# One index table, an unchecked first index, a wait before the second-layer weight requests, and nine warm-up products

## The chip, the cores and the metric

The kernel runs on one core of one Trainium2 chip. The metric is the device time in microseconds of one execution, the median of several. TensorE (PE) does the matrix products; VectorE (DVE), ScalarE (ACT) and GpSimd (POOL) prepare operands and empty the result banks; SyncE (SP) and ScalarE issue the DMA requests, and the profile lists what their queues do as SPq and ACTq.

## The reference

For each of the two samples b, x is 1024 tokens by 256 features. Each sample picks one of 64 weight matrices for layer 0, and one of 3 expert MLPs for layer 1; two further MLPs are shared.

```python
x = x + (einsum('bsd,bdh->bsh', x, W[cat_ids]) + b[cat_ids][:, None, :])
s0, s1 = relu(x @ swi[0]) @ swo[0], relu(x @ swi[1]) @ swo[1]
eo = relu(x @ wi[type_label]) @ wo[type_label]          # type_label: one of 3 per sample
gate_in = concatenate([eo[:, 0], s0[:, 0], s1[:, 0]], axis=-1)
w = softmax(relu(gate_in @ g1) @ g2, axis=-1)[:, :, None, None]
x = x + eo * w[:, 0] + s0 * w[:, 1] + s1 * w[:, 2]
```

## The kernel before

Everything lies feature-major: 128 partitions hold features, 512 tokens are one tile's columns, and a sample has two tiles (t) of two feature halves (d). A product in f32 accuracy is made of three products of rounded operands: high by high, high by low and low by high. So each operand is first rounded (`x_hi`, `w_hi`, `m_hi`, `h_hi`, mostly by ACT), and the remainder is then taken (`x_lo`, `w_lo`, `m_lo`, `h_lo`, by DVE or POOL). Nothing is scheduled by a compiler: each engine's instructions stand in a written order, and semaphores hold the engines together.

**TensorE's order.** `WARMUP` = 10 products of `ones` into the bank `left` (L912), which nobody reads; `layer0_first` (sample 0, tile 0: 12 products of 512 columns), `layer0(0, 1)` (12 more, both on L739); `direct_first` (the first group of the MLP's hidden units, L782); `direct(1, i)` (the second group, L730, i = 0 to 3 into left, chain, corner, right); `layer0(1, 0)` and `layer0(1, 1)`; eight `output(0, u)`; and then the long loop over groups 2 to 23. `direct(1, i)` waits for `h_lo` number i of group 0, for they share a bank. `output(0, 4)` starts a bank that `make_x1(1, 1, 0)` on DVE must have emptied (L508).

**SP's order.** It loads the first index (`value_load`, L237, a read of a table in device memory), issues two requests for layer 0's weights `w_raw` and one for the bias (`load_layer0(0)`); loads the first expert index (L246); requests the weights of group 0 (`wo`) and group 1 (`wi`, `wo`), 256 KB each (L194, L201); requests sample 1's four halves of x, 256 KB each (L188, `load_x(sp, 1, t, d)`); and then does `load_layer0(1)`. From group 2 on it waits for a staging buffer to come free.

**ACT's order.** It requests x's first half (0, 0, 0), loads the expert index for itself (L410), and requests (0, 0, 1); once the first half has landed, it requests x's second tile, (0, 1, 0) and (0, 1, 1); it rounds `w_hi`, requests group 0's `wi` (L194), and goes on rounding. In the stretch that the prediction speaks of, its order is `hidden_hi(0, 0)`, `x_hi_of(1, 0, 0)`, `hidden_hi(0, 1)`, `x_hi_of(1, 0, 1)`, `hidden_hi(0, 2)`, `split_first_hi(0, True)`, `hidden_hi(0, 3)`, `w_hi_of(1, d)`. `x_hi_of` waits until that half of x has landed.

**DVE's order.** After `hidden_lo(0, i)` come `w_lo_of(1, d)`, `x_lo_of(1, 1, d)`, `make_x1(1, 0, 0)`, `hidden_lo(1, 0)`, `make_x1(1, 0, 1)`, `hidden_lo(1, 1 to 3)`, `make_x1(1, 1, 0)`, `make_x1(1, 1, 1)`.

Of the kernel before, what the change touches and what calls it, by code (L numbers as in the profile page):

```python
# [14 lines left out]
DC = 2  # L15
SHARED = 2
GROUPS = 4
DIRECT = 2
WARMUP = 10
SLOTS = 3  # L20

SQ = 32
# [21 lines left out]
NTH = [1, 3, 2, 4]  # L44

def build(nc, x_t, cat_w, cat_b, mlp_w, mlp_ids, cat_ids, g1, g2, out_t):
    B, _, _, S = x_t.shape
    D = DC * P
    HALVES = S // TOK  # L50
    CATS = cat_w.shape[0]
    BANKS = mlp_w.shape[0]
    EXPERTS = BANKS - SHARED
    assert B == 2 and HALVES == 2

    with ExitStack() as ctx:
# [6 lines left out]
        def sem(name):  # L63
            return ctx.enter_context(nc.semaphore(name))
# [57 lines left out]
        x_loaded = [[[sem(f"x_loaded{b}{t}{d}") for d in range(DC)] for t in range(HALVES)] for b in range(B)]  # L122
# [49 lines left out]
        def x1_part(b, t, d):  # L172
            return x1[:, b, t, d, :]
# [13 lines left out]
        def load_x(eng, b, t, d):  # L187
            eng.dma_start(x1_part(b, t, d), x_t[b][:, d, t * TOK:(t + 1) * TOK]).then_inc(x_loaded[b][t][d], 16)  # L188
# [7 lines left out]
        def load_group(eng, bank, j):  # L196
            if j < DIRECT:

                if j:
                    load_wi(eng, bank, j)  # L200
                eng.dma_start(staged[:, j % 2, WO:A11], group_weights(bank, j, slice(WO, A11))).then_inc(wo_loaded[j], 16)  # L201
            else:
                eng.dma_start(staged[:, j % 2, 0:RAW_S], group_weights(bank, j, slice(0, RAW_S))).then_inc(staged_loaded[j % 2], 16)
# [10 lines left out]
        def second_part(j):  # L214
            return DIRECT + j + 1 if j < DIRECT else 2 * j + 2
# [18 lines left out]
        @block.sync  # L234
        def _(sp):
            def load_layer0(b):
                cat = sp.value_load(cat_ids[0:1, b:b + 1], min_val=0, max_val=CATS - 1)  # L237
                for d in range(DC):
                    sp.dma_start(w_raw[:, b, d * D:(d + 1) * D], cat_w[bass.ds(cat, 1), :, d].rearrange("a p n -> p (a n)")  # L239
                                 ).then_inc(w_loaded[b][d], 16)  # L240
                sp.dma_start(bias[:, b, :], cat_b[bass.ds(cat, 1)].rearrange("a p d -> p (a d)")).then_inc(bias_loaded[b], 16)

            load_layer0(0)
            for q, (kind, _) in enumerate(PASSES):
                if kind == 0:
                    mlp = sp.value_load(mlp_ids[0:1, q:q + 1], min_val=0, max_val=EXPERTS - 1)  # L246
                    bank = bass.ds(mlp, 1)
                else:
                    bank = slice(EXPERTS + kind - 1, EXPERTS + kind)
                for j in range(q * GROUPS, (q + 1) * GROUPS):  # L250
                    if j >= 2:

                        sp.wait_ge(m_split, second_part(j - 2))
                    load_group(sp, bank, j)
                    if j == 1:
                        for t in range(HALVES):
                            for d in range(DC):
                                load_x(sp, 1, t, d)
                        load_layer0(1)
                if q == 0:  # L260

                    sp.wait_ge(layer0_done, B * HALVES * DC)
                    sp.dma_start(g1_sb[:], g1).then_inc(g_loaded, 16)
                    for d in range(DC):
                        sp.dma_start(g2_sb[:, d, :, :], g2[:, d, :].rearrange("(a c) k -> c a k", c=SQ)).then_inc(g_loaded, 16)

            for b in range(B):
                sp.wait_ge(added[b][0], 3)
                sp.dma_start(out_t[b, :, :, 0:TOK], x1[:, b, 0, :, :]).then_inc(out_written, 16)
            for n, (b, t) in enumerate(PAIRS[PASSES[-1][1]]):  # L270
                for d in range(DC):
                    sp.wait_ge(last_added, n * DC + d + 2)
                    columns = slice(0, TOK // 2 if n * DC + d == 2 * DC - 1 else TOK)
                    sp.dma_start(out_t[b, :, d, t * TOK:(t + 1) * TOK][:, columns], x1_part(b, t, d)[:, columns]
                                 ).then_inc(out_written, 16)
            sp.wait_ge(out_written, 16 * (B + 2 * DC + 1))
# [70 lines left out]
        def _(act):  # L347
# [59 lines left out]

            act.wait_ge(ones_ready, 1)
            nc.scalar.activation(table[:], ones[:, 0:1], ACT.Relu)
            mlp = act.value_load(mlp_ids[0:1, 0:1], min_val=0, max_val=EXPERTS - 1)  # L410

            load_x(act, 0, 0, 1)
            act.wait_ge(x_loaded[0][0][0], 16)
# [35 lines left out]
            for j in range(DIRECT, N):  # L449
# [21 lines left out]
                q = j // GROUPS - 1  # L471
# [24 lines left out]
            b, t = PAIRS[PASSES[-1][1]][1]  # L496
# [229 lines left out]
        def _(pe):  # L726
# [183 lines left out]
            pe.wait_ge(ones_ready, 1)  # L910
            for _ in range(WARMUP):
                nc.tensor.matmul(left[:, 0:P], ones[:], ones[:], start=True, stop=True)  # L912
# [72 lines left out]
```

## Time and profile before

| | before |
|---|---|
| device time, median of 3 runs | 268.43 us (268.33 to 268.64) |
| the profiled execution, its own time | 268.28 us |
| its span, first to last instruction | 266.4 us |
| TensorE busy | 262.2 us, 98% of the span |
| weight loads (PEld), DVE, ACT, POOL busy | 217.4, 162.7, 150.0, 162.1 us |
| share of TensorE in the chain that ended last | 97% |
| granted TensorE clock, mean | 1.000 |

The profiled execution's time is 1.9 us more than its span. A row of the timeline is: start, duration, engine, line, operation, what is written from what, shapes, and in brackets the idle time of the engine before it with what ended that. Instructions of an engine overlap a little in these rows, because each is shown from its start to the end of its last write.

### The profile page before, as it was taken

To read this page: it belongs to the slowest core of one execution; us is meant where nothing else is said; L and a number is where in the kernel's file an instruction comes from. 1 tells how busy PE (TensorE), PEld (TensorE's weight loads), DVE (VectorE), ACT (ScalarE), POOL (GpSimd) and SP (SyncE) were. 2 spreads that over 40 slices of the span, in tenths; PEclk is the share of its full clock that TensorE was granted. 3 is DMA by queue.
4 is the path that set the end of the run, shared out by engine and by line. 5 is a ranking of instruction groups with operands and counts; after the bars stand their busy time and mean duration, and the time that the engine had idled before them with its cause. 6 is when DMAs were issued, how large, how long until landed. Compare 5 with 4: busy or idle time off the path is not lost.

```text
span 266.4 us, 3466 instructions
## 1 busy us (share of the span) xinstructions
PE 262.2 (98%) x1160; PEld 217.4 (82%) x1160; DVE 162.7 (61%) x246; ACT 150.0 (56%) x266; POOL 162.1 (61%) x171
## 2 busy tenths in 40 slices
PE   8999999999999999999999999999999999999995
PEld 7788888888888888888888888888888888888884
DVE  3879968635645435644445565345477577985664
ACT  2696357866666555565655744646645755645320
POOL 0379999999958949838944725725626528535000
PEclk9999999999999999999999999999999999999999
DMA  5844322112012112202022112012022022000404
GB/s 154 235 162 160 119 79 80 28 55 80 16 65 79 38 41 79 79 5 79 0 81 79 20 58 81 9 73 79 2 79 79 0 79 80 1 0 0 157 4 158
DMA packets 7473, 18.31 MB, mean 69 GB/s; under 512 B 1312, under 2 KB 2080, under 8 KB 7456
## 3 DMA queue, kind: packets, MB, share of 16 engines
q1 hardware_dynamic: 6592, 16.65, 18.7%
q10 hardware_dynamic: 864, 1.44, 1.7%
q8 instruction: 9, 0.15, 0.2%
q14 instruction: 8, 0.07, 0.1%
HBM read 16.00 MB, written 2.10 MB: 68 GB/s over the span
## 4 chain that ended last, share of the span: by engine, by line
PE 97%; DMA 1%; SPq 1%; issue 0%; DVE 0%; ACT 0%; DVEq 0%
PE acc L730 49%; PE chain L730 23%; PE right L730 12%; PE left L730 6%; PE acc L739 4%; DMA w_raw<-cat_w 1%; SPq L237 1%; PE left L782 1%; PE corner L730 1%; PE right L782 1%; PE corner L782 1%; PE chain L782 1%; DVE x L721 0%; ACT w_hi L373 0%; SPq L239 0%
## 5 line engine op out<-in xcount | busy, mean ns | idle before, releaser
L281 POOL TENSOR_TENSOR m_lo<-staged,m_hi 128x512 fp32r<-128x512 f32 (+2 forms) x49 | 82.9, 1702 | 76.3 <-ACT m_hi L361 62.8
L730 PE MATMUL acc<-h_hi,m_hi 128*128 128x512 f32 x190 | 73.9, 389 | 0.0
L730 PE MATMUL acc<-h_hi,m_lo 128*128 128x512 f32 x190 | 73.9, 389 | 0.0
L730 PE MATMUL acc<-h_lo,m_hi 128*128 128x512 f32 x190 | 73.9, 389 | 0.0
L385 ACT COPY kept<-chain 128x512 f32<-128x512 f32 x66 | 38.9, 589 | 52.8 <-PE chain L730 52.7
L730 PEld LDWEIGHTS acc<-h_lo,m_hi 128*128 128x128 f32 x190 | 35.7, 188 | 7.5
L730 PEld LDWEIGHTS acc<-h_hi,m_lo 128*128 128x128 f32 x190 | 35.7, 188 | 7.4
L730 PEld LDWEIGHTS acc<-h_hi,m_hi 128*128 128x128 f32 x190 | 35.7, 188 | 7.3
L517 DVE SCALAR_TENSOR_TENSOR h_lo<-left,h_hi 128x512 fp32r<-128x512 f32 x24 | 16.6, 690 | 28.4 <-ACT h_hi L397 28.4
L281 POOL TENSOR_TENSOR staged<-staged 128x128 f32<-128x128 f32 x66 | 30.9, 482 | 1.7
L522 DVE TENSOR_TENSOR left<-left,kept 128x512 f32<-128x512 f32 x22 | 15.3, 694 | 23.7 <-PE left L730 23.7
L517 DVE SCALAR_TENSOR_TENSOR h_lo<-corner,h_hi 128x512 fp32r<-128x512 f32 x24 | 16.6, 691 | 16.3 <-ACT h_hi L397 16.3
L522 DVE TENSOR_TENSOR corner<-right,kept 128x512 f32<-128x512 f32 x22 | 15.4, 699 | 17.9 <-ACT kept L385 17.9
L730 PE MATMUL chain<-t_hi,m_lo 128*128 128x512 f32 x66 | 25.7, 389 | 0.0
L730 PE MATMUL chain<-t_hi,m_hi 128*128 128x512 f32 x66 | 25.7, 389 | 0.0
L730 PE MATMUL chain<-t_lo,m_hi 128*128 128x512 f32 x66 | 25.7, 389 | 0.0
L397 ACT ACTIVATE h_hi<-right 128x512 fp32r<-128x512 f32 x24 | 14.4, 600 | 19.2 <-DVE right L522 18.8
L397 ACT ACTIVATE h_hi<-corner 128x512 fp32r<-128x512 f32 x24 | 14.4, 600 | 18.5 <-DVE corner L522 18.5
L361 ACT CAST m_hi<-staged 128x896 fp32r<-128x896 f32 x22 | 20.8, 944 | 0.0
L517 DVE SCALAR_TENSOR_TENSOR h_lo<-right,h_hi 128x512 fp32r<-128x512 f32 x24 | 16.6, 691 | 3.5 <-ACT h_hi L397 0.8
L281 POOL TENSOR_TENSOR t_lo<-t_raw,t_hi 128x512 fp32r<-128x512 f32 x12 | 15.3, 1298 | 2.5 <-ACT t_hi L404 2.5
L517 DVE SCALAR_TENSOR_TENSOR h_lo<-chain,h_hi 128x512 fp32r<-128x512 f32 x24 | 16.3, 680 | 0.4 <-ACT h_hi L397 0.4
(149 smaller groups left out, 439.0 us busy)
## 6 DMA issues: line engine op xcount, KB each, us to landing
staged<-mlp_w SPq DMA_DIRECT2D x22, 512.0 KB, 3.3
x<-x_t ACTq DMA_DIRECT2D x4, 256.0 KB, 3.4
x<-x_t SPq DMA_DIRECT2D x4, 256.0 KB, 6.9
out_t<-x SPq DMA_DIRECT2D x2, 512.0 KB, 4.4
staged<-mlp_w SPq DMA_DIRECT2D x3, 256.0 KB, 3.6
g_sb<-g SPq DMA_DIRECT2D x1, 768.0 KB, 3.8
out_t<-x SPq DMA_DIRECT2D x3, 256.0 KB, 2.3
w_raw<-cat_w SPq DMA_DIRECT2D x4, 128.0 KB, 2.9
```

Of the source, the lines that this page charges most:

```text
L237: cat = sp.value_load(cat_ids[0:1, b:b + 1], min_val=0, max_val=CATS - 1)
L281: return nc.gpsimd.tensor_tensor(out, a, b, ALU.subtract)
L361: nc.scalar.copy(m_hi[:, j % SLOTS, 0:PLAIN], staged[:, j % 2, 0:PLAIN]).then_inc(m_hi_ready, 1)
L385: nc.scalar.copy(kept[:, n, :], chain[:]).then_inc(kept_ready, 1)
L397: nc.scalar.activation(h_hi[:, j % 2, i, :], hidden[i][:], ACT.Relu).then_inc(h_hi_ready, 1)
L517: nc.vector.scalar_tensor_tensor(out=h_lo[:, j % 2, i, :], in0=hidden[i][:], scalar=0.0, in1=h_hi[:, j % 2, i, :].bitcast(F32), op0=ALU.ma ...
L522: nc.vector.tensor_tensor(out[:], product[:], kept[:, n, :], ALU.add).then_inc(hidden_ready, 1)
L730: last = nc.tensor.matmul(out[:, columns], half[:, slot, at:at + P], moving[:, columns], start=(start and n == 0), stop=(stop and n == 2), ...
L739: return nc.tensor.matmul(acc[t][d][:], w[:, b, at:at + P], x_part(x, b, t, i), start=start, stop=stop)
L782: return nc.tensor.matmul(hidden[i][:], w[:, 0, at:at + P], moving, start=start, stop=stop, skip_group_check=True)
```

## The change

One table `ids` holds the two layer-0 indices and then the two expert indices, in place of `cat_ids` and `mlp_ids`, and the expert indices are now read at a nonzero offset. The layer-0 index is loaded without bounds. SP waits for the second half of x's second tile before its first request for group 0's weights, and with it before all its further requests. There are 9 warm-up products in place of 10.

```diff
-WARMUP = 10
+WARMUP = 9
...
             def load_layer0(b):
-                cat = sp.value_load(cat_ids[0:1, b:b + 1], min_val=0, max_val=CATS - 1)
+                cat = sp.value_load(ids[0:1, b:b + 1])
...
                 if kind == 0:
-                    mlp = sp.value_load(mlp_ids[0:1, q:q + 1], min_val=0, max_val=EXPERTS - 1)
+                    mlp = sp.value_load(ids[0:1, B + q:B + q + 1], min_val=0, max_val=EXPERTS - 1)
...
                 for j in range(q * GROUPS, (q + 1) * GROUPS):
+                    if j == 0:
+
+                        sp.wait_ge(x_loaded[0][1][DC - 1], 16)
                     if j >= 2:
...
-            mlp = act.value_load(mlp_ids[0:1, 0:1], min_val=0, max_val=EXPERTS - 1)
+            mlp = act.value_load(ids[0:1, B:B + 1], min_val=0, max_val=EXPERTS - 1)
...
-        "mlp_ids": np.asarray(itok_B_0_2)[None],
-        "cat_ids": np.asarray(itok_B_0_63)[None],
+
+        "ids": np.concatenate([np.asarray(itok_B_0_63), np.asarray(itok_B_0_2)])[None],
```

## Rows read from the trace of the kernel before

**Rows 1.** The page: the span in 40 slices, TensorE and its clock.

```profile
PE   8999999999999999999999999999999999999995
PEclk9999999999999999999999999999999999999999
```

**Rows 2.** The chain of work that ended last, by time: start, length, what.

```profile
2.49 0.05 SPq L239
...
2.65 2.57 DMA w_raw<-cat_w
...
5.25 0.41 ACT w_hi L373
...
5.79 5.88 PE acc L739 x24
```

**Rows 3.** Line L237 from 0 to 3 us: duration ns least/median/most, start.

```profile
L237 SPq TENSOR_LOAD <-cat_ids_ptr x1: 859/859/859, 0.7 to 0.7; - x1
L237 SPq TENSOR_LOAD <-cat_ids x1: 524/524/524, 1.6 to 1.6; - x1
L237 SPq FUSED_REGOPS  x1: 181/181/181, 2.2 to 2.2; - x1
L237 SPq SEQ_ASSERT  x1: 28/28/28, 2.4 to 2.4; - x1
```

**Rows 4.** Line L246, the expert index on SP, whole span.

```profile
L246 SPq TENSOR_LOAD <-mlp_ids_ptr x2: 1448/1690/1933, 4.2 to 29.4; - x2
L246 SPq ALU_OP  x1: 41/41/41, 31.3 to 31.3; - x1
```

**Rows 5.** The timeline, 6.7 to 9 us, layer 0's operands and SP's requests.

```profile
6.73 0.69 DVE L504 TENSOR_TENSOR x_lo<-x,x_hi 128x512 fp32r<-128x512 f32 x1
7.38 0.34 SPq L201 DMA_DIRECT2D staged<-mlp_w  x1
7.74 0.62 PE L739 MATMUL acc<-x_lo,w_hi 128*128 128x512 f32 x2
8.28 0.62 ACT L369 CAST x_hi<-x 128x512 fp32r<-128x512 f32 x1 [0.28 <-DMA x<-x_t]
```

**Rows 6.** Line L912, the warm-up, whole span.

```profile
L912 PE MATMUL left<-ones x20: 341/421/579, 1.1 to 5.3; 128*128 128x128 f32 x20
```

**Rows 7.** Line L201 at 8.4 us, group 1's `wo`: its request and landing.

```profile
L201 SPq DMA_DIRECT2D staged<-mlp_w x1: 332/332/332, 8.4 to 8.4; - x1
...
DMA to landing us min/median/max: 4.0/4.0/4.0
```

**Rows 8.** Line L188 at 8.8 us, sample 1's first half of x, likewise.

```profile
L188 SPq DMA_DIRECT2D x<-x_t x1: 432/432/432, 8.8 to 8.8; - x1
...
DMA to landing us min/median/max: 6.7/6.7/6.7
```

**Rows 9.** Windows of 1 us: PE, PEld, DVE, ACT, POOL, clock, DMA share, GB/s.

```profile
12.00:13.00 1.00, 1.00 (x6) 0.84 (x5) 1.00 (x2) 0.39 (x1) 0.52 (x1) 1.00 0.73 123
```

**Rows 10.** The timeline, 14.4 to 18.3 us: the way from x to `direct(1, 1)`.

```profile
14.40 0.62 ACT L354 CAST m_hi<-staged 128x512 fp32r<-128x512 f32 x1
14.92 0.59 ACT L397 ACTIVATE h_hi<-left 128x512 fp32r<-128x512 f32 x1
15.49 0.62 ACT L369 CAST x_hi<-x 128x512 fp32r<-128x512 f32 x1
16.02 0.59 ACT L397 ACTIVATE h_hi<-chain 128x512 fp32r<-128x512 f32 x1
16.64 0.69 DVE L517 SCALAR_TENSOR_TENSOR h_lo<-chain,h_hi 128x512 fp32r<-128x512 f32 x1 [0.41 <-ACT h_hi L397]
18.11 0.19 PEld L730 LDWEIGHTS chain<-part_hi,m_hi 128*128 128x128 f32 x1
```

**Rows 11.** The timeline, 28.9 to 30.4 us: the way to `output(0, 4)`.

```profile
28.91 0.74 DVE L508 SCALAR_TENSOR_TENSOR x<-acc,bias,x 128x512 f32<-128x512 f32 x1
30.34 0.19 PEld L730 LDWEIGHTS acc<-h_hi,m_hi 128*128 128x128 f32 x1
```

More of the change, by code:

```diff
@@ L44, with build @@
 NTH = [1, 3, 2, 4]
-def build(nc, x_t, cat_w, cat_b, mlp_w, mlp_ids, cat_ids, g1, g2, out_t):
+def build(nc, x_t, cat_w, cat_b, mlp_w, ids, g1, g2, out_t):
     B, _, _, S = x_t.shape
@@ L50, in build @@
     HALVES = S // TOK
-    CATS = cat_w.shape[0]
     BANKS = mlp_w.shape[0]
```

## The prediction

> **What bounds the kernel now.** I read the page first: TensorE is at nine tenths or more in every slice between the first and the last, and its clock column is full throughout [rows 1]. So no other engine bounds it; time can be won or lost only where TensorE starts, where it pauses, and at the end. The chain of waits says the same with times: it is SP's work and a transfer of `w_raw` up to 5.22 us, a cast on ACT from 5.25 to 5.66, and from 5.79 TensorE to the end [rows 2]. The change touches the way to 5.79 and the order of the transfers behind it. A 128x512 product follows the last after 0.227 us (the row at 7.74 has two that end 0.62 later, 0.39 being one's own length [rows 5]). The 24 products of layer 0's first sample take 5.88 us [rows 2] where 24 x 0.227 = 5.45, so some 0.4 us of pauses lie in that stretch. After that I find none: whatever comes late by less than its slack costs nothing, whatever comes later shifts the whole rest.
>
> **The first index without its assertion.** SP reads a pointer (0.859 us), reads the index (0.524), then runs a FUSED_REGOPS of 0.181 and a SEQ_ASSERT of 0.028 [rows 3]; its address arithmetic starts at 2.49 and the request goes out at 2.65 [rows 2]. The read ends at about 0.73 + 0.86 + 0.03 + 0.52 = 2.14. Without the last two, the arithmetic can start at 2.18, which saves 0.31. The lower bound is 0.07 (SEQ_ASSERT and its gap alone, if the FUSED_REGOPS were needed); I take 0.31, since the address arithmetic has an instruction of its own at 2.49. `w_raw` would then land at 4.91, `w_hi` be done at 5.35, and the first product start at 5.48, 0.31 earlier.
>
> **One table.** Line L246 reads its pointer twice, once per load, from the same table [rows 4], so a load never reuses a pointer that the queue has read; one table saves no read. What it adds is an offset: the expert load at offset 0 has no ALU_OP, the one at offset 1 has one of 41 ns [rows 4], about 0.08 us with its gaps. Both expert loads at 4.2 us and on ACT now get one. On SP it is hidden behind the new wait. On ACT it stands ahead of the request of x's half (0, 0, 1), which then lands 0.08 later, or 0.2 to 0.3 later if layer 0's second `w_raw` request, now sent first, takes its place in the DMA engines.
>
> That half is needed: `x_lo` of it runs from 6.73 to 7.42, and TensorE uses it at 7.74 [rows 5]. With TensorE 0.31 earlier it is wanted at 7.43 and is there at 7.42 + 0.08 + about 0.1 for the semaphore. So of 0.31 some 0.15 is left behind this stage; 0 to 0.31 are the bounds.
>
> **Nine warm-up products.** Twenty passes (each of the ten f32 products is two) begin at 1.1 and the last at 5.3, its 341 ns bringing it to 5.61 [rows 6]. Ten would hold a first product at 5.48 up by 0.13; the passes are (5.3 - 1.1) / 19 = 0.22 apart, so nine products end 0.44 earlier, at 5.2, and free the engine in time. Taken alone, this edit is worth 0 in the kernel before, since the cast ends later than the warm-up [rows 2, 6]. What it may cost is the clock. The last pass takes 341 ns where the others take 421 [rows 6], as if it alone had run partly at a higher clock; I read that as TensorE at its lower level, 1.2 GHz, until about 5.4 us, although the clock column shows full speed there [rows 1]. I price this among the rivals. The Trainium skill, page "TensorE: Matmul & The Clock Gate", Part 1, says that the default state is throttled and that activity releases the throttle; the trace agrees, and the rule speaks against every warm-up product that is taken away. By that rule the sum would be the clock rival's time if the shorter activity no longer suffices, and mine if it does.
>
> **The wait before SP's further requests.** This is the part I price highest. SP's first request for group 0's `wo` goes out at 7.38 [rows 5]. Now it waits for x's half (0, 1, 1), whose landing ends ACT's wait at 8.28 [rows 5]. Waking and the usual 0.16 from address arithmetic to request [rows 2] bring it to 8.45 to 8.5: +1.05 to 1.1. Everything behind it on SP shifts: `wo` of group 0; `wi` and `wo` of group 1; sample 1's four halves of x; the second `load_layer0` with its pointer read, two weight requests and bias. What it buys is nothing that I can find: ACT casts x's half (0, 1, 0) before 8.28 and (0, 1, 1) by 8.90, and TensorE, four products after the pair at 7.74 [rows 5], reaches the first at 8.65 and the second four products on, at 9.56. Even 0.3 earlier it would not wait for them.
>
> The first of sample 1's halves is asked for at 8.8 and lands 6.7 later, at 15.5 [rows 8]. ACT casts it at 15.49, directly then: the instruction before it starts at 14.92 and they follow each other by 0.52 otherwise (14.40 to 14.92) [rows 10], so ACT would have begun at 15.44. This transfer has 0.05 of slack on ACT. Does a later request land just as much later? Between 12 and 13 us the DMA engines were at a share of 0.73 and moved 123 GB/s [rows 9], so bytes are not all that holds it, and fewer bytes in flight ahead will not bring it forward by much. Yet `wo` of group 1, asked for 0.4 earlier, landed after 4.0, at 12.4 [rows 7], so up to 6.7 - 4.0 = 2.7 us of this landing is not owed to its distance in the queue and might shrink. Bounds: 0.5 and 1.1; I take 1.0, near the requests' own shift, because the stretch with a low rate lies behind the requests and not ahead of them.
>
> Then ACT's cast runs at 16.5, and `hidden_hi(0, 1)`, queued behind it, at 17.0 in place of 16.02; `h_lo` from 17.65 to 18.35 in place of 16.64 to 17.33. TensorE's weight load for `direct(1, 1)` waits for it and stands at 18.11 [rows 10]: slack 18.11 - 17.33 = 0.78. So it is late by 1.0 - 0.78 = 0.22 against before, and all of the start's gain is gone with it. DVE carries the delay on, since it is back to back from 19.3 to 30 us: `make_x1(1, 1, 0)` ends at 29.65 and the load for `output(0, 4)` stands at 30.34 [rows 11], slack 0.69, late by 0.31. These are not added: the later one includes the earlier. A shift of the groups' weights costs nothing: the last of them lands at 12.4 [rows 7] and ACT casts group 1's from 14.40 [rows 10], 2 us of cover. Layer 0's weights for sample 1 come about a microsecond later too, but ACT casts them behind `hidden_hi(0, 3)` and reaches them as much later itself; with ACT on time they would be the next to be late.
>
> **Sum.** The end moves by the larger of two: minus the start's gain (-0.15), and the delay of x less its slack (1.0 - 0.69 = +0.31). I forecast +0.3: a span of 266.7 us, and 268.28 + 0.3 = 268.6 us for the time. The profiled execution was 0.15 under the median of the runs, so against that median the forecast is +0.2 to +0.3. A measurement of this kernel tells 0.2% (0.54 us) from no change; this is within it.
>
> **The rivals.**
>
> *The transfers close up* (25%). If the queue behind SP absorbs 0.4 us or more, x is late by 0.6 or less and never reaches TensorE; then the gain at the start stays, 268.28 - 0.15 = 268.1, and 267.97 if all of 0.31 stays. For it: this x takes 6.7 us [rows 8] where `wo` ahead of it takes 4.0 [rows 7]. Against it: the low rate at 12 us [rows 9].
>
> *The clock rises late* (8%). Place: the pause between the last warm-up pass at 5.2 and the first product at 5.48, where before it was 5.61 to 5.79. It decides if the level had not risen at 5.4 for want of the tenth product. Then the products of layer 0 run at half speed, 0.45 in place of 0.227 each. If the rise needs as long a stretch again as the warm-up's 4.3 us, 2.2 us are lost less the pauses; if it comes after half of that, 1.1. Time 269.4 to 270.5, with 269.9 between.
>
> *x comes later still* (12%). The second pointer read or a slower landing puts the delay at 1.25 us or more: 268.28 + 0.56 = 268.9 to 269.2. It decides from a delay of 1.23.
>
> *More pauses close at the start* (5%). If x and w land earlier because SP keeps its requests back, up to 0.31 + 0.4 of pauses are won: 267.6 to 267.9.
>
> *The change has no effect at all* is what is left near 268.3 in the forecast's and the first rival's cases, when the delay comes to about 0.7.
>
> **How the numbers follow.** Forecast 50%, with its own range 268.35 to 268.85; transfers close up 25%; clock 8%; x still later 12%; pauses 5%. Faster by over 0.2% (under 267.9): 0.06. Slower by over 0.2% (over 268.97): the clock, most of the later x, 0.18. The same: 0.76. The range from 267.95 to 269.1 leaves out the clock, part of the fourth and little else.
>
> **What would show it.** Line L237's SEQ_ASSERT gone for the first load and the first product near 5.5, against 5.79; an ALU_OP on ACT's queue before its second x request; L201's first request near 8.45; ACT's cast of x at 16.4 to 16.6 in place of 15.49; a wait of TensorE's weight load near 18.1 or 30.3 for DVE. I am wrong if TensorE's products after 5.5 us follow each other by 0.45, if `w_raw`'s request does not move, or if the transfers of sample 1's x land before 16.1.

## The result and the profile after

| | before | after |
|---|---|---|
| median of 22 executions each, one comparison | 268.61 us | 269.64 us |
| lowest and highest | 268.24, 271.07 | 269.03, 270.36 |
| ratio, 95% interval | | 1.0038 (1.0026 to 1.0049) |
| span of the profiled execution | 266.4 us | 268.4 us |
| TensorE busy | 262.2 us | 263.8 us |

The chain of waits of the changed kernel up to its first group, as start, length, what (it answers to [rows 2]):

```profile
0.74 0.39 ACTq L187
...
1.17 1.28 ACT L411
...
3.08 0.58 ACTq L412
...
3.96 0.35 ACTq L187
...
4.34 0.44 ACTq L187
...
4.82 0.45 ACTq L187
...
5.31 0.41 ACT w_hi L375
...
5.86 7.86 PE acc L741 x24
13.72 0.23 PE left L784
```

The chain used to run over SP's queue and the landing of `w_raw`. Now it runs over ACT's: the first weights are there (asked for at 2.40, they took 2.1 us), but the cast `w_hi` stands behind ACT's three late requests for x. The first product starts at 5.86 against 5.79, although the assertion is gone. Then layer 0's 24 products take 7.86 us against 5.88. From `direct_first` on nothing is lost: 268.4 - 13.7 = 254.7 us are left in the changed kernel and, with 5.79 + 5.88 = 11.67, 266.4 - 11.7 = 254.7 in the kernel before. All of the 2.0 us of this profile lie in the first 13.7.

ScalarE's index load, line L412 of the changed kernel, and SyncE's, L236, to 3 us (duration ns least/median/most, start; [rows 3] shows SyncE's before):

```profile
L412 ACTq TENSOR_LOAD <-ids_ptr x1: 1717/1717/1717, 1.2 to 1.2; - x1
L412 ACTq ALU_OP  x1: 69/69/69, 3.0 to 3.0; - x1
L412 ACTq TENSOR_LOAD <-ids x1: 584/584/584, 3.1 to 3.1; - x1
```

```profile
L236 SPq TENSOR_LOAD <-ids_ptr x1: 863/863/863, 0.7 to 0.7; - x1
L236 SPq TENSOR_LOAD <-ids x1: 581/581/581, 1.6 to 1.6; - x1
```

The same line of the kernel before, L410 there:

```profile
L410 ACTq TENSOR_LOAD <-mlp_ids_ptr x1: 932/932/932, 1.2 to 1.2; - x1
```

The pointer read that ScalarE starts at 1.2 us now takes 1.72 us in place of 0.93. So x's half (0, 0, 1), queued behind it, is asked for at 3.96 us, not 2.95. The timeline of TensorE and its neighbours in the changed kernel answers to [rows 5]:

```profile
5.86 1.19 PE L741 MATMUL acc<-x_hi,w_hi 128*128 128x512 f32 x2 [0.59 <-ACT w_hi L375]
6.85 1.05 PE L741 MATMUL acc<-x_lo,w_hi 128*128 128x512 f32 x2
7.42 0.43 DVE L630 CAST x_hi<-x 128x512 fp32r<-128x512 f32 x1 [1.25 <-DMA x<-x_t]
...
8.55 1.05 PE L741 MATMUL acc<-x_hi,w_hi 128*128 128x512 f32 x2
9.41 0.99 PE L741 MATMUL acc<-x_lo,w_hi 128*128 128x512 f32 x2
9.44 0.62 ACT L371 CAST x_hi<-x 128x512 fp32r<-128x512 f32 x1 [0.80 <-DMA x<-x_t]
9.58 0.34 SPq L200 DMA_DIRECT2D staged<-mlp_w  x1
```

Two things are to be seen. x's half (0, 0, 1) ends DVE's wait at 7.42; in the kernel before `x_lo` of it already ran at 6.73. And a pair of products takes 1.05 us where [rows 5] has 0.62: from 5.86 to 10.2 they follow each other by 0.43 us, which is TensorE at its lower level, 1.2 GHz (before, they follow each other by 0.227). The clock column has 1.00 in this stretch as in every other (start and end, length, then busy time of PE, PEld, DVE, ACT and POOL, clock, DMA share, GB/s):

```profile
5.80:13.50 7.70, 7.64 (x24) 6.00 (x25) 4.58 (x9) 2.99 (x7) 0.96 (x2) 1.00 0.67 223
```

### The profile page after: what moved, and what is told of

Its sections match the earlier page's. It is cut to its first block, busy times and chain, and to the rows that moved or that the text cites. A ratio compares the mean times of both kernels' runs of the same rounds, so it can differ in the third digit from the quotient of the medians.

```text
span 268.4 us, 3460 instructions
## 1 busy us (share of the span) xinstructions
PE 263.8 (98%) x1158; PEld 218.5 (81%) x1158; DVE 163.1 (61%) x246; ACT 149.9 (56%) x266; POOL 162.3 (60%) x171
## 4 chain that ended last, share of the span: by engine, by line
PE 97%; ACTq 1%; ACT 1%; issue 0%; DVE 0%; DVEq 0%
PE acc L732 48%; PE chain L732 23%; PE right L732 12%; PE left L732 6%; PE acc L741 5%; ACTq L187 1%; PE left L784 1%; PE chain L784 1%; PE corner L732 1%; PE right L784 1%; PE corner L784 1%; ACT L411 0%; ACTq L412 0%; DVE x L723 0%; ACT w_hi L375 0%
## 5 line engine op out<-in xcount | busy, mean ns | idle before, releaser
L399 ACT ACTIVATE h_hi<-right 128x512 fp32r<-128x512 f32 x24 | 14.4, 599 | 19.2 <-DVE right L524 18.8
L399 ACT ACTIVATE h_hi<-corner 128x512 fp32r<-128x512 f32 x24 | 14.4, 600 | 18.5 <-DVE corner L524 18.5
```

Of the source, the lines that this page charges most:

```text
L399: nc.scalar.activation(h_hi[:, j % 2, i, :], hidden[i][:], ACT.Relu).then_inc(h_hi_ready, 1)
```

## The experiments

Each ran in 12 executions, beside 35 of the kernel before. The medians of before were 268.59 (E1 to E4), 268.56 (E5 to E8) and 268.62 (E9 to E12). "At 270 or above" counts executions; the kernel before had 5 or 6 such of 35 each time.

| | kernel | median us | ratio (95%) | at 270 or above | (0, 0, 1) asked for, landed, us | 
|---|---|---|---|---|---|
| E1 | before, 9 products | 268.43 | 0.9987 (0.9952 to 1.0021) | 2 | 2.96, 6.2 |
| E2 | after, 10 products | 269.44 | 1.0018 (0.9991 to 1.0045) | 0 | 4.19, 7.4 |
| E3 | before, one table | 269.44 | 1.0021 (0.9984 to 1.0058) | 1 | 3.82, 7.4 |
| E4 | after, two tables | 268.89 | 0.9991 (0.9962 to 1.002) | 0 | 3.03, 7.3 |
| E5 | before, no assertion on SP | 268.92 | 1.002 (0.9995 to 1.0044) | 1 | 2.95, 6.8 |
| E6 | before, SP's wait | 268.50 | 1.0009 (0.9977 to 1.004) | 2 | 2.95, 6.2 |
| E7 | after, a copy for ACT | 268.88 | 0.9999 (0.9976 to 1.0021) | 0 | 3.04, 7.5 |
| E8 | before, x asked for first | 269.06 | 1.0011 (0.9979 to 1.0042) | 2 | 1.17, 4.6 |
| E9 | before, 7 products | 269.92 | 1.0023 (0.9991 to 1.0054) | 5 | 2.94, 6.4 |
| E10 | after, 12 products | 269.35 | 1.0003 (0.9978 to 1.0028) | 0 | 3.92, 7.4 |
| E11 | after, once more | 269.22 | 1.001 (0.9987 to 1.0033) | 1 | 3.88, 7.6 |
| E12 | before, no assertion on SP and ACT | 268.61 | 0.9992 (0.9959 to 1.0024) | 2 | 2.67, 6.0 |

No interval here excludes 1. What carries the reading is the profile's rows, and how the single executions lie: all 12 of E3 are above 269.1, where 28 of the 35 of before are below that. Of the 48 executions with one shared table (E2, E3, E10, E11) 47 are at 269.0 or above, of the 105 of before 29. The changed kernel's own median is 269.64 in one comparison and 269.22 in another (E11), so a single difference of 0.3 or 0.4 us is weak evidence; E4, E5 and E7, at 0.30 to 0.36 over before, support each other.

**E1, the ninth product alone.**

```diff
-WARMUP = 10
+WARMUP = 9
```

> The kernel before with 9 warm-up products and nothing else. In the changed kernel's profile TensorE's products followed each other by 0.427 us up to 10.2 us, where before they were at 0.227 from the first. Clock theory (the tenth product is what brings the rise of the clock ahead of layer 0): the products at half speed are seen here too, and the time is 0.7 to 2.0 us over before. Rival, the index theory (all of the loss is x landing a microsecond late, as ACT's pointer read took 1.72 us in place of 0.93): no change within 0.1 us, since x's requests are those of before.

268.43, no loss. In its profile the clock had risen before layer 0, although TensorE paused for 0.62 us there. So the missing tenth product does not by itself make it late.

**E2, the change with the tenth product back.**

```diff
-WARMUP = 9
+WARMUP = 10
```

> The changed kernel with 10 warm-up products. Clock theory: layer 0's products follow each other by 0.227 again; what is left of the loss is what the late x costs, so 0 to 1.0 us over before. Index theory: about 1 us over before in any case, as in the changed kernel. If both are right and add, 0.5 to 1.0 over before and 0.3 to 1.0 under the changed kernel.

269.44: 0.85 over before remains, 0.2 less than in the changed kernel, and none of 12 executions is at 270. The index theory's side. The 0.2 is no effect of the tenth product that could be relied on, as E11 shows.

**E3, one table alone.**

```diff
-                cat = sp.value_load(cat_ids[0:1, b:b + 1], min_val=0, max_val=CATS - 1)
+                cat = sp.value_load(ids[0:1, b:b + 1], min_val=0, max_val=CATS - 1)
...
-                    mlp = sp.value_load(mlp_ids[0:1, q:q + 1], min_val=0, max_val=EXPERTS - 1)
+                    mlp = sp.value_load(ids[0:1, B + q:B + q + 1], min_val=0, max_val=EXPERTS - 1)
...
-            mlp = act.value_load(mlp_ids[0:1, 0:1], min_val=0, max_val=EXPERTS - 1)
+            mlp = act.value_load(ids[0:1, B:B + 1], min_val=0, max_val=EXPERTS - 1)
```

> The kernel before with one table of indices and nothing else (the assertion, the 10 products and SP's order are kept). Index theory: ACT's pointer read takes 1.6 to 1.8 us in place of 0.93, x's half (0, 0, 1) is asked for near 4.0 in place of 2.95 and TensorE pauses for it: 0.6 to 1.1 us over before. Rival (the slow pointer read in the one profile was chance): 0 to 0.1 over before, with the ALU_OP of 0.07 us as all that is new.

269.44, +0.85. ScalarE's index load, and TensorE's pause for x in the chain of waits:

```profile
L410 ACTq TENSOR_LOAD <-ids_ptr x1: 1691/1691/1691, 1.2 to 1.2; - x1
```

```profile
3.82 3.56 DMA x<-x_t
...
7.41 0.44 DVE x_hi L628
...
7.89 4.77 PE acc L739 x18
```

The products here follow each other by 0.23 from the second pair on, and TensorE pauses 0.48 us for x, so this +0.85 is x's.

**E4, the change with two tables.** The two tables of before put back; the unchecked load, the wait and the 9 products stay.

> The changed kernel with the two tables of before. Index theory: ACT's pointer read is back near 0.93, x's halves land at 6.2, 7.3 and 8.3, SP's wait ends near 8.3; the time is 0.3 to 1.0 under the changed kernel. Clock theory: if the clock still rises late in the profile, the time stays 0.5 to 1.5 over before, as with 9 products alone. Wait theory (sample 1's x lands 1 us late and TensorE pauses at 18.1 or 30.3): such a pause of 0.2 to 0.3 us is seen if the clock rose early.

268.89: 0.75 of the change's loss is gone with the table. The clock was up in time. There was no pause at 18 or 30 us. But TensorE again waited for x, which I had expected to land at 6.2:

```profile
3.03 4.27 DMA x<-x_t
...
7.33 0.44 DVE x_hi L631
...
7.80 4.78 PE acc L742 x18
```

Asked for in time, x's half took 4.27 us to land where it had taken 3.3 before.

**E5, the assertion alone.**

```diff
-                cat = sp.value_load(cat_ids[0:1, b:b + 1], min_val=0, max_val=CATS - 1)
+                cat = sp.value_load(cat_ids[0:1, b:b + 1])
```

> The kernel before with the layer-0 index loaded without its assertion, and nothing else. Reordering theory (from the changed kernel with two tables, where the second weight request, sent at 3.0 with x's half (0, 0, 1) sent at the same time, landed a microsecond earlier than before and x a microsecond later): the weights land near 4.9 and 5.5, x's half at 7.0 to 7.4 in place of 6.2, the 25th product starts near 12.4 and the time is 0.3 to 0.9 us over before. Rival (the assertion's 0.3 us is simply saved): 0.15 to 0.3 under before.

268.92, +0.36, at the low end of the reordering theory's range. The weights were asked for 0.32 earlier, and x's half landed later:

```profile
2.33 0.95 SPq L239 DMA_DIRECT2D w_raw<-cat_w  x2
```

```profile
2.95 3.89 DMA x<-x_t
...
6.86 0.44 DVE x_hi L628
...
7.34 4.78 PE acc L739 x18
```

x's request at 2.95 is that of before; its transfer takes 3.89 in place of 3.3. The second weight request is sent at about 2.9, right beside it and no longer 0.3 behind. It did not land earlier itself, as I had expected (6.65 us, 6.62 before), so the order of the two in the DMA engines is not shown, only that x lands later.

**E6, SP's wait alone.**

```diff
+                    if j == 0:
+
+                        sp.wait_ge(x_loaded[0][1][DC - 1], 16)
```

> The kernel before with SP's wait for x's second tile, and nothing else. Wait theory, from the prediction: SP's first request for wo goes from 7.4 to 8.45, sample 1's first half of x lands near 16.5, TensorE pauses near 18.1 or 30.3 for 0.2 to 0.35 us: 0.2 to 0.35 over before. Rival (the landing of sample 1's x does not follow its request, as it landed at 13.9, 14.5 and 14.9 in three of the runs so far): no change within 0.1.

268.50, no loss. SP's queue and ACT's casts behind it:

```profile
8.30 0.34 SPq L201 DMA_DIRECT2D staged<-mlp_w  x1
...
9.71 1.86 SPq L188 DMA_DIRECT2D x<-x_t  x4
```

```profile
14.88 0.59 ACT L400 ACTIVATE h_hi<-left 128x512 fp32r<-128x512 f32 x1
15.36 0.61 ACT L372 CAST x_hi<-x 128x512 fp32r<-128x512 f32 x1
```

The requests are 0.9 later, and sample 1's first half of x is cast at 15.36, earlier than the 15.49 of before [rows 10]. The four halves landed 4.9 to 5.4 us after their requests, the first at 4.9 and not 6.7.

**E7, a copy of the table for ScalarE.**

```diff
-            mlp = act.value_load(ids[0:1, B:B + 1], min_val=0, max_val=EXPERTS - 1)
+            mlp = act.value_load(act_ids[0:1, B:B + 1], min_val=0, max_val=EXPERTS - 1)
```

> The changed kernel, but ScalarE reads its index from a second copy of the same table, with the same offset. If the pointer read of 1.7 to 2.1 us comes of two queues reading one table's pointer at about the same time, it is back near 0.93 to 1.0 and the time is that of the changed kernel with two tables, 268.9, 0.7 under the changed kernel. Rival (it is the joint table's offset or its place in memory): the read stays at 1.7 or more and the time at 269.6.

```profile
L412 ACTq TENSOR_LOAD <-act_ids_ptr x1: 912/912/912, 1.2 to 1.2; - x1
```

268.88, the time of E4, and the read is back at 0.91, with the offset and the joint layout kept. So it is the sharing of the table with SyncE, which reads the same pointer from 0.73 us on, that slows the read; whether the two reads must lie that close in time was not tried. That the time is E4's again does not mean that x set the pace again. Here the second half of the weights took longest, and TensorE waited for it:

```profile
2.94 4.74 DMA w_raw<-cat_w
...
7.70 0.41 ACT w_hi L375
...
8.24 4.55 PE acc L741 x18
```

x's half had landed at 7.5.

**E8, x's half (0, 0, 1) asked for ahead of the index load.**

```diff
             load_x(act, 0, 0, 0)
+            load_x(act, 0, 0, 1)
...
-            load_x(act, 0, 0, 1)
```

> The kernel before with ScalarE's request for x's half (0, 0, 1) moved ahead of its index load, right behind the first request. If x's half is what sets the pace of layer 0, its landing moves from 6.2 to about 4.5 to 5 and weights land in its wake, near 5.2 to 5.8: 0.1 to 0.4 us under before. Rival (the second weight transfer sets the pace, or the early x delays the first weights): no change or up to 0.3 over.

269.06, +0.5: a miss. ScalarE's pointer read came to stand at 1.7 us, took long in spite of a table of its own, and x's second tile was asked for at 4.26 and set the pace:

```profile
L411 ACTq TENSOR_LOAD <-mlp_ids_ptr x1: 1667/1667/1667, 1.7 to 1.7; - x1
```

```profile
4.26 4.09 DMA x<-x_t
...
8.38 0.63 ACT x_hi L369
...
9.05 3.03 PE acc L739 x12
```

So a slow pointer read has a second cause too, transfers in flight or the moment. Which, stays open.

**E9, seven products.**

```diff
-WARMUP = 10
+WARMUP = 7
```

> The kernel before with 7 warm-up products, which leaves TensorE idle from about 4.0 to 5.4 us. Clock theory (a pause ahead of layer 0 makes executions likelier in which the clock rises only after several products): more than 3 of 12 executions at 270 us or above, against about 11 in 70 of the kernel before, and a median up by 0.3 to 2. Rival (what decides is when an execution happens to start, whatever the warm-up does within a microsecond): as many slow ones as before, the median within 0.15.

Five of 12 at 270 or above, the median 269.92. Its profile shows the late clock with x in time; the pause was 2.03 us:

```profile
6.45 1.19 PE L739 MATMUL acc<-x_hi,w_hi 128*128 128x512 f32 x2 [2.03 <-ACT w_hi L373]
7.43 1.06 PE L739 MATMUL acc<-x_lo,w_hi 128*128 128x512 f32 x2
```

The span was 268.8, 2.4 over before, the longest of all these profiles. Not all of it is the clock's:

```profile
2.65 3.23 DMA w_raw<-cat_w
...
6.45 7.68 PE acc L739 x24
```

The 24 products took 7.68 us in place of 5.88, 1.8 more. The other 0.66 were lost before them: the first weights, asked for at 2.65 as before, took 3.23 us in place of 2.57.

**E10, twelve products in the changed kernel.**

```diff
-WARMUP = 9
+WARMUP = 12
```

> The changed kernel with 12 warm-up products, which end near 6.1 us, so that no pause is left ahead of layer 0. Clock theory: no execution above 269.9, the median 269.3 to 269.5, since x's half lands at 7.4 in any case and hides the later first product. Rival (the executions at 270 and above come from something else): as many of them as in the changed kernel, 7 in 22.

269.35, the highest at 269.87. As the clock theory says; but the unchanged kernel had only one of 12 at 270 beside it (E11), so these 12 do not decide between the two.

**E11, the changed kernel once more.** No edit.

> The changed kernel once more. Clock theory: some 3 or 4 of 12 executions at 270.0 to 270.4, the others at 269.0 to 269.7; a profile in which the clock rises before 7 us has a span of about 267.4, one in which it rises near 10 has 268.4. Index theory: ACT's pointer read 1.6 to 2.1 us again.

269.22 and one of 12 at 270, where 3 or 4 were expected and the first comparison had 7 of 22. Over before it is 0.60 this time, not 1.03. The profile had a span of 267.6 and the level rose within layer 0's first tile (pairs of 1.05, then of 0.63 us):

```profile
5.78 1.05 PE L741 MATMUL acc<-x_hi,w_hi 128*128 128x512 f32 x2 [0.51 <-ACT w_hi L375]
6.67 0.63 PE L741 MATMUL acc<-x_lo,w_hi 128*128 128x512 f32 x2
```

The pointer read was 1.70. What of the 2.0 us in the first profile is x's is read from E10, where x's half was asked for at 3.92 and landed at 7.4 as there, and all products ran at full pace: its first group starts at 12.70 against 11.67. So about 1.0 is x's and 1.0 the clock's.

**E12, both assertions away.**

```diff
-                cat = sp.value_load(cat_ids[0:1, b:b + 1], min_val=0, max_val=CATS - 1)
+                cat = sp.value_load(cat_ids[0:1, b:b + 1])
...
-            mlp = act.value_load(mlp_ids[0:1, 0:1], min_val=0, max_val=EXPERTS - 1)
+            mlp = act.value_load(mlp_ids[0:1, 0:1])
```

> The kernel before with the layer-0 index on SyncE and the expert index on ScalarE both loaded without their assertions. Reordering theory: x's half (0, 0, 1) is asked for at 2.70 and the second weight request at 2.93, so the order of before is kept and x lands near 6.0: 0.1 to 0.4 us under before, and 0.5 to 0.8 under the kernel with SyncE's assertion alone removed (268.92). Rival (whatever is sent for weights earlier delays x): as with SyncE's alone, 0.3 to 0.4 over before.

268.61, neither a gain nor a loss, where 0.1 to 0.4 were to be gained; 0.3 under E5. x's half landed at 5.99, 0.25 earlier, but the first weights took longer:

```profile
2.33 3.33 DMA w_raw<-cat_w
...
5.68 0.41 ACT w_hi L373
...
6.23 1.86 PE acc L739 x7
```

3.33 us in place of 2.57 [rows 2]. That x's earlier request is the reason is not shown: E9's first weights took 3.23 with no request moved. None of these kernels is faster than the one before by more than chance.

## Why the prediction was wrong, by its steps

**One table, priced at 0.08 us, costs 0.85.** This is the step that failed first. I read the row of a pointer read twice from the same table as "no read is saved" and counted the ALU_OP. I did not ask what two queues do that read one table's pointer at the same time: SyncE from 0.73 to 1.59, ScalarE from 1.2. What it cost is not the 0.08 us of the ALU_OP but the 0.8 us of the longer pointer read, which stands ahead of x's half. The read took 0.91 to 1.01 us in eight profiles with separate tables (E8, whose request order is another, is the exception at 1.67), and 1.69 to 2.06 in the five with a shared one. Why it is slow is not shown. None of my rivals had this. The measured 269.64 lies within the clock rival's 269.4 to 270.5, but by luck: E2, E3 and E10 reach 269.35 to 269.44 with products that in their profiles run at full pace but for the first pair at most.

**The assertion, priced at a gain of 0.15, costs 0.36 when taken away on SP alone.** The 0.31 us were saved on SP's queue as worked out (the first request at 2.31 to 2.40 in place of 2.65). The step that failed is what x pays. I had named the delay of x's half, 0.08 and up to 0.3 with the order turned, and then took 0.08; its landing moved by 0.6 in E5, 1.06 in E4 and 1.3 in E7. The prediction also had the path wrong. It followed the first half of the weights and x, and left out the second half, on which the first tile's remaining products wait. In the kernel before, it is this half that ended ACT's wait:

```profile
6.64 0.41 ACT L373 CAST w_hi<-w_raw 128x256 fp32r<-128x256 f32 x1 [0.99 <-DMA w_raw<-cat_w]
```

It landed at 6.62 there and at 6.65 in E5, though asked for 0.32 earlier, so in that profile the 0.15 were not to be had even with x in time. (In E4 it landed at 5.5, in E7 at 7.7.)

**SP's wait, priced as the decisive +0.3, costs nothing.** In E6 the requests moved by 0.9, where 1.05 to 1.1 were forecast, but the landing did not follow them. (In the changed kernel they moved by 2.2, to 9.58, x's second tile being late itself.) 6.7 us was one draw: the same half landed at 13.9 to 14.9 in E1, E3, E6, E8, E9 and E12, and at 15.7 in E5, where it was asked for at 9.44. Taken from a single row, with the transfers ahead of it in the queue at 3.1 to 4.0 and those behind it at 6.8 to 7.2, it should have had its low bound at nothing. In the changed kernel sample 1's first half lands at 16.4 and is cast at 17.45, ACT being late itself, so no wait is seen.

**The ninth product, priced at nothing beyond the clock.** Alone it costs nothing (E1), which holds. The clock rival stood at 8% and named the place, the pause before the first product. In the changed kernel the late x requests keep ACT from casting `w_hi`, so the pause is 0.5 to 0.6 us (E11 and the first profile) and 8 of 34 executions are at 270 or above; with one table and 10 or 12 products (E2, E3, E10) it is 1 of 36, and with 9 and separate tables (E1, E4, E7) 2 of 36. That the short warm-up and the late x act together is what these counts suggest; they do not show it. The kernel before has such executions as well, 5 or 6 of 35; 270 lies 1.4 over its median and only 0.4 to 0.8 over that of the kernels with one table, so the counts do not compare like with like; and a pause alone is not enough, for it was 0.62 us in E1's profile and 0.87 in E8's, with the products at full pace behind it.

**The sum.** One table +0.85, the assertion +0.36, the wait and the ninth product -0.06 and -0.16: +1.0 by the single parts, and +1.03 was measured. That the two agree is luck, for the parts do not add. E2 is E3 without the assertion and with the wait, and both have the median 269.44; x's half landed at 7.4 in both, and the 18 products behind it start alike, at 7.89 in E3 and in E2 at 7.87:

```profile
7.87 4.77 PE acc L741 x18
```

Once the table makes x late, the assertion and the wait cost nothing more. The second weights land at 5.2 us in both, so they no longer share the time of x's transfer for long; that this is the reason was not tested. In the other order, E4 has all but the table and is 0.30 over before, and the table's return is worth 0.75. What lies between E2's +0.85 and +1.03 is no more than the changed kernel's own two medians differ, 269.64 and 269.22, so a share of the ninth product is not measured. (The 268.6 us of the forecast is the profiled execution's 268.28 plus 0.3; on the median of 268.43 it would be 268.7.) That the pauses behind layer 0 close to nothing, and that an early loss shifts the whole rest, was right: 254.7 us on both sides.

## What to carry to other kernels

Where TensorE is full to the end, every microsecond of the start counts at full price, and the start is then a race of small reads and transfers: price an edit there by each request that is queued behind it on every engine, and follow every operand that the first products wait for. Do not let two queues read one small table's pointer at about the same time; separate tables, or a copy, cost nothing here. Costs that end in the same wait do not add: test them together before summing them. A landing time of one transfer in one profile is one draw, and a forecast that hangs on it needs its neighbours' times as its other bound.

## What the runs showed that I had not expected

- Two queues on one table: the second pointer read took 1.69 to 2.06 us against 0.91 to 1.01; a copy of the table brought it back to 0.91.
- With `w_raw` asked for 0.3 us earlier, x's half took 3.89, 4.27 and 4.46 us (E5, E4, E7; its request moved by 0.1 at most), where it took 3.2 to 3.4 in the four profiles that have both requests at their old times (before, E1, E6, E9). With x asked for 0.28 earlier too it took 3.3 again (E12).
- The first weights took 2.2 to 3.2 us in those four profiles with nothing moved that stands ahead of them.
- The profile's clock column read 1.00 while products of 512 columns ran 0.43 us apart. The pace of the products tells the level there, not the column.
- The Trainium skill, page "TensorE: Matmul & The Clock Gate", Part 1, says that the moment of the rise varies from run to run with the same kernel. That agrees with the two profiles of the changed kernel, where the products were at half speed up to 10.2 us in the one and for the first two only in the other.
